# Scatter of the expert coefficients in two row tiles, and the weighing on VectorE straight out of PSUM

## The chip, the cores and the metric
The kernel runs on one core of one Trainium2 chip. The metric is the device time of one execution in microseconds (us), the median of the runs; lower is better.

## The reference, cut to what matters
Four stages follow each other on an activation of 4 x 256 tokens of 256 features: cross attention, a feed-forward layer with five-bit quantised weights, a gated expert layer with int8 quantisation, and a product-key expert layer. The change touches the last one alone.

```
q = (x @ Wq).reshape(b, t, H, 2, DK)                 # H=4 heads, DK=64
sim1 = einsum('bthd,hkd->bthk', q1, keys[:, :, 0])   # 128 keys a side
sim2 = einsum('bthd,hkd->bthk', q2, keys[:, :, 1])
s1, i1 = top_k(sim1, 8);  s2, i2 = top_k(sim2, 8)
all_scores  = s1[..., :, None] + s2[..., None, :]    # 8 x 8 pairs
all_indices = i1[..., :, None] * 128 + i2[..., None, :]
final_scores, pk_idx = top_k(all_scores, 8)
hidden = silu(x . e_down[idx]) * relu(final_scores)
out    = sum over 32 chosen experts of hidden * e_up[idx]
```

There are 2048 experts, and an index beyond them is clamped to the last.

## The kernel before, in words
The five engines run hand-written instruction lists, each in its own order, and meet at semaphores. The 1024 tokens are eight tiles of 128 (t = 0 to 7, `NT = 8`), two to a batch b (`B = 4`). The last expert layer gathers nothing. For each batch TensorE computes the inner product of every token with all 2048 rows of e_down, in eight steps called `experts`, and ScalarE writes silu of them as G (`gate`). An expert is numbered 16 x i + e, i from 0 to 127 and e from 0 to 15 (`EROWS`); G, and the coefficients PR, are laid out as [partition i, e, token].

The coefficients are made dense for a tile by one-hot matmuls, `scatter`. Before it VectorE has found each token's 32 choices (`top8`, `pair_top8`, `look_up`), and transposed them so that the 128 partitions are four slots of 32 tokens (s) times 32 choices, with 32 columns (g): token = 32 s + g. The coefficient is split in three bf16 parts whose sum is the f32 value. For each g, TensorE multiplies a stationary one-hot over i (`oh`, 128 x 128) with a moving one-hot over (slot, e), 4 x 16 = 64 columns, times the part (`wc`), and sums the three parts in PSUM: 96 matmuls a tile, in four quarters of 24, in banks 2 and 3 by turns. `slot16` adds 16 times the slot to the column index. `mask` and `one_hots` make msk (2048 elements a partition), oh (4096) and wc: two parts on VectorE, the third by `third_one_hots` on GpSimd.

For tiles 0 to 4 (`DVE_WEIGHS = NT - 3 = 5`) ScalarE copies each quarter out of PSUM into PR (`coefficients_out`, L1055) and GpSimd multiplies it by G (`weigh`, L381). For tiles 5 to 7 VectorE does both at once (L1495). Then `up` multiplies PR with e_up, sixteen matmuls (L728), and `result` adds the token's residual and lets it be stored.

These steps are woven with the gated expert layer (names with `c_`) of batch b + 2, whose steps go to and fro between TensorE, VectorE and ScalarE. The loop over b has two passes (b = 0 and 1); tiles 4 to 7 come behind it, the tail. TensorE's list in a pass: `sims(b, 1)`, `scatter(b, 0)`, `pre` (transposes of the next batch's tokens), `c_x_transposed`, `half_queries` (L668), `experts`, `c_factors`, `up(b, 0)`, ..., `sims(b + 1, 0)`, `c_first`, `scatter(b, 1)`, `experts`, ... , `up(b, 1)`. VectorE's: `top8`, `c_ratio` (first at L1309), `pair_top8`, `c_factor` (L1317), `look_up`, `c_round` (L1331), `mask`, `c_clip` (L1347), `one_hots`, `c_h`, `result`, `c_a`, then the same again for the next tile with `c_ratio2` (L1369), `c_factor2` (L1379), `c_round2`, `c_clip2` (L1352), and at the end `x3` and `ln_apply` (L1158). ScalarE: `tokens_out`, `queries`, `c_root` (L967), which `c_factor` waits for, `c_diag`, gates, and so on.

## Time and profile before

| | us |
|---|---|
| median of 3 runs | 459.7 (458.96 to 460.38) |
| profiled execution, its own time | 458.2 |
| span of its trace | 456.4 |
| TensorE matmuls busy | 374.5 (82%) |
| VectorE busy | 360.9 (79%) |
| ScalarE busy | 248.4 (54%) |
| GpSimd busy | 196.8 (43%) |

The numbers below are from one execution, in us from the start of its span. A row of a timeline merges neighbours of one kind: its start, its length, engine, line, operation, tiles and count; in square brackets stands the idle time of the engine before it and whose instruction ended it. An f32 matmul shows as two instructions, so x16 of them are eight calls. PE is TensorE, DVE is VectorE, ACT is ScalarE, POOL is GpSimd.

### The profile page before, as it was taken

How to read it: one execution, taken by the hardware profiler on the slowest of the kernel's cores; microseconds unless marked ns; L12 is line 12 of the kernel's file. 1: busy time of each engine (PE TensorE's matmuls, PEld its weight loads, DVE VectorE, ACT ScalarE, POOL GpSimd, SP SyncE). 2: the span in 40 equal slices, each digit the busy share in tenths (PEclk: the TensorE clock that was granted, in tenths of full speed). 3: DMA queues.
4: the chain of work that ended last, by engine and by line, in shares of the span. 5: the costliest groups of instructions: out<-in, count | busy, mean ns of one | idle time of the engine just before them, and what ended most of it. 6: DMA issues, size and time to landing. Idle time of an engine off the chain costs nothing.

```text
span 456.4 us, 6956 instructions
## 1 busy us (share of the span) xinstructions
PE 374.5 (82%) x2510; PEld 283.6 (62%) x2510; DVE 360.9 (79%) x878; ACT 248.4 (54%) x371; POOL 196.8 (43%) x211
## 2 busy tenths in 40 slices
PE   2987897599799988988388679978799878789486
PEld 1554664244345448987267568867688667688475
DVE  4998699958986956267947977698969799999991
ACT  4789959789788880136555254675475645012000
POOL 2355844479889993000011441353523325414220
PEclk9998999989989998998759968999999999979799
DMA  9910000000000004000000000000000000000000
GB/s 264 362 53 2 0 1 0 0 2 0 0 2 0 0 2 159 27 2 0 0 2 1 0 1 1 1 12 1 13 0 14 1 1 14 1 13 0 2 24 11
DMA packets 11138, 11.32 MB, mean 25 GB/s; under 512 B 608, under 2 KB 10592, under 8 KB 11104
## 3 DMA queue, kind: packets, MB, share of 16 engines
q1 hardware_dynamic: 11104, 10.88, 7.4%
q8 instruction: 20, 0.33, 0.3%
q14 instruction: 14, 0.11, 0.1%
HBM read 9.83 MB, written 1.05 MB: 24 GB/s over the span
## 4 chain that ended last, share of the span: by engine, by line
DVE 38%; PE 35%; ACT 13%; issue 9%; POOL 4%; DMA 1%; DVEq 0%; POOLq 0%; ACTq 0%
PE pair L728 6%; PE pair L559 5%; DVE arena L1480 5%; PE pair L697 5%; POOL arena L332 3%; PE pair L519 3%; PE pair L715 3%; PE pair L668 3%; PE pair L497 2%; PE pair L526 2%; DVE arena L1223 2%; DVE arena L1477 1%; DVE arena L1495 1%; PE pair L397 1%; DVE i L1422 1%
## 5 line engine op out<-in xcount | busy, mean ns | idle before, releaser
L332 POOL TENSOR_TENSOR arena<-arena 128x512 f32<-128x512 f32 x64 | 91.0, 1432 | 52.0 <-ACT arena L930 21.5
L697 PE MATMUL pair<-arena,EDT 128*128 128x256 f32 x256 | 59.5, 384 | 3.0 <-ACT arena L1063 3.0
L728 PE MATMUL pair<-EU,arena 128*128 128x256 f32 x256 | 57.8, 380 | 2.8 <-DVE arena L1502 1.6
L1223 DVE TENSOR_REDUCE arena<-arena 128x16 f32<-128x512 f32 x64 | 42.7, 679 | 20.2 <-POOL arena L332 20.1
L519 PE MATMUL pair<-QP,nidentr 128*128 128x512 f32 x144 | 47.6, 456 | 12.5 <-ACT arena L930 9.9
L369 POOL TENSOR_TENSOR arena<-arena,ctxT 128x2048 bf16<-128x2048 bf16 x8 | 34.8, 4351 | 46.9 <-DVE arena L1471 39.6
L697 PEld LDWEIGHTS pair<-arena,EDT 128*128 128x128 f32 x256 | 47.7, 191 | 9.9 <-ACT arena L1063 3.6
L728 PEld LDWEIGHTS pair<-EU,arena 128*128 128x128 f32 x256 | 47.9, 190 | 9.2 <-DVE arena L1495 3.1
L715 PE MATMUL pair<-arena 128*128 128x64 bf16 x768 | 30.4, 203 | 18.8 <-DVE arena L1495 9.4
L519 PEld LDWEIGHTS pair<-QP,nidentr 128*128 128x128 f32 x144 | 27.3, 203 | 24.4 <-issue 16.6
L1063 ACT ACTIVATE arena<-pair 128x512 f32<-128x512 f32 x32 | 18.7, 595 | 42.0 <-PE pair L697 41.9
L715 PEld LDWEIGHTS pair<-arena 128*128 128x128 bf16 x768 | 28.2, 104 | 21.5 <-DVE arena L1495 10.0
L381 POOL TENSOR_TENSOR arena<-arena 128x512 f32<-128x512 f32 x20 | 24.9, 1274 | 38.5 <-ACT arena L1055 38.5
L526 PE MATMUL pair<-arena 128*128 128x512 fp8e4 x128 | 40.4, 399 | 0.0
L933 ACT ACTIVATE arena<-pair 128x1024 f32<-128x1024 f32 x32 | 33.3, 1042 | 12.4 <-PE pair L526 12.4
L930 ACT ACTIVATE arena<-pair,sq_bias 128x1024 f32<-128x1024 f32 x32 | 36.2, 1131 | 5.9 <-PE pair L526 4.8
L1218 DVE TENSOR_SCALAR arena<-arena 128x1024 fp8e4<-128x1024 f32 x32 | 33.1, 1036 | 6.2 <-PE pair L526 3.7
L915 ACT ACTIVATE arena<-arena,clip_bias 128x1024 fp8e4<-128x1024 f32 x32 | 37.2, 1165 | 0.0
L559 PE MATMUL pair<-arena 128*128 128x128 f32 x256 | 32.8, 292 | 2.7 <-POOL arena L315 2.4
L559 PEld LDWEIGHTS pair<-arena 128*128 128x128 f32 x256 | 32.1, 208 | 3.5 <-issue 2.9
L497 PE MATMUL pair<-arena 128*128 128x512 f32 x64 | 30.9, 605 | 0.0
L1480 DVE TENSOR_TENSOR arena<-arena,ctxT 128x2048 bf16<-128x2048 bf16 x16 | 29.0, 1852 | 0.0
(196 smaller groups left out, 686.1 us busy)
## 6 DMA issues: line engine op xcount, KB each, us to landing
arena<-in_L_ffn_e_down_dram SPq DMA_DIRECT2D x1, 2048.0 KB, 12.2
EU<-in_L_ffn_e_up_dram SPq DMA_DIRECT2D x1, 2048.0 KB, 8.1
arena<-in_L_ffn_w_fc_dram SPq DMA_DIRECT2D x2, 512.0 KB, 5.3
X<-in_x_dram SPq DMA_DIRECT2D x1, 1024.0 KB, 6.0
arena<-in_L_ffn_w_proj_dram SPq DMA_DIRECT2D x1, 1024.0 KB, 13.7
GUW<-in_fside_BxS2xS_dram SPq DMA_DIRECT2D x1, 1024.0 KB, 11.4
out_dram<-arena SPq DMA_DIRECT2D x8, 128.0 KB, 1.7
CTX<-in_ctx_dram SPq DMA_DIRECT2D x1, 512.0 KB, 5.0
```

The lines of the kernel that those rows point to most:

```text
L332: pool.tensor_tensor(qf(g), sq[:, :, 0:32], sq[:, :, 32:64], ALU.add).then_inc(s["folded"], 1)
L497: last = pe.matmul(bank[2 + i % 2], W1T[:, k, m * P:m * P + P], xnT[:, k, half * 512:half * 512 + 512], start=(k == 0), stop=(k == 1))
L519: pe.matmul(to[half], nidentr[:, :], QP[:, c % 2, part, cols[half]], start=(part == 0), stop=False)
L526: last = pe.matmul(to[half], stepI[:, j, :], qr[:, g % QDEEP, cols[half]], start=False, stop=True, skip_group_check=kept)
L559: last = pe.matmul(bk2(F2_BANK[b])[:, n, o * P:o * P + P], h2T[:, k, at:at + P], W2T[:, k, o * P:o * P + P], start=(k == 0), stop=(k == HI ...
L697: last = pe.matmul(bk2(4 + i % 2)[:, r, :], EDT[:, k, at:at + P], xT4[:, b % 2, k, :], start=(k == 0), stop=(k == 1))
L715: last = pe.matmul(bank[2 + q % 2][:, g8 * 64:g8 * 64 + 64], oh[:, g // NG, :, g % NG], wc[:, c, g // NG, :, g % NG], start=(c == 0), stop ...
L728: last = pe.matmul(bk2(7)[:, n, :], PR[:, n, e, :], EU[:, e, :], start=(e == 0), stop=(e == EROWS - 1))
L915: act.activation(qr[:, g % QDEEP, :], qu[:, g // NS % 2, :], ACT.Relu, bias=clip_bias[:, 0:1], scale=-GRID / STEPS[g % NS], saturate=False ...
L930: act.activation(qd[g % 3], pair[2 + g % 2][:, :], ACT.Square, bias=sq_bias[:, g % NS:g % NS + 1]).then_inc(s["squared"], 1)
L1223: dve.tensor_reduce(err[:, g // NS % 2, :, g % NS], qf(g), AX.X, ALU.add).then_inc(s["reduced"], 1)
L1480: ins = dve.tensor_tensor(wc[:, c], msk, over(t, 2 + c, 64), ALU.mult)
```

## The change: what it does
- One scatter matmul becomes two, over partitions 0 to 63 and 64 to 127 of the same operands, each into a bank of its own. Each needs only its two slots, so the moving side is 2 x 16 = 32 columns (`JW`) in place of 64. A tile has 192 matmuls, in two halves of 96 with one wait ahead of each, in place of 96 in four quarters. `slot16` holds 0 or 16.
- msk shrinks to 1024 elements a partition, wc to 3 x 1024. VectorE makes all three parts of wc in one instruction; `third_one_hots` goes.
- `coefficients_out` (ScalarE) and GpSimd's `weigh` go. VectorE multiplies PSUM by G into PR for all eight tiles: two halves a tile, two instructions each.
- The second half of a tile goes into the banks of the first, so it waits for VectorE's products of the first half. For tiles 6 and 7 the second half has banks 4 and 5.
- The order: TensorE has `scatter(b, 0, 0)` before `pre`, and `scatter(b, 0, 1)` before `half_queries`; `scatter(b, 1, 1)` one `experts` step after its first half; in the tail `scatter(B-2, 1, 1)` stands inside `experts(B-1, 2..8)`. VectorE has `weigh(t, 0)` behind `top8` of the next tile and `weigh(t, 1)` behind its `pair_top8`.

```diff
-            def third_one_hots(t):
-                pool.wait_ge(s["d_mask"], t + 1)
...
-                pool.tensor_tensor(wc[:, 2], msk, part.unsqueeze(2).to_broadcast([P, NO, 64, NG]),
-                                   ALU.mult).then_inc(s["d_onehot_p"], 1)
...
+            def scatter(b, n, half):
                 t = 2 * b + n
+                if half == 0:
+                    pe.wait_ge(s["d_onehot"], t + 1)
+                if t == NT - 1:
+                    pe.wait_ge(s["d_weighed"], 4 * (t - 1) + 2 * half + 2)
+                elif t == NT - 2 and half == 1:
+                    pe.wait_ge(s["d_g_e"], 8 * B)
+                elif t or half:
+                    pe.wait_ge(s["d_weighed"], 4 * t + 2 * half)
+                for g16 in range(16):
+                    g = 16 * half + g16
+                    for c in range(3):
+                        for r in range(2):
+                            rows = slice(64 * r, 64 * r + 64)
+                            last = pe.matmul(bank[scatter_bank(t, half) + r][:, g16 * JW:g16 * JW + JW],
+                                             oh[rows, g // NG, :, g % NG], wc[rows, c, g // NG, :, g % NG],
+                                             start=(c == 0), stop=(c == 2))
+                last.then_inc(s["d_c_t"], 2)
...
-            def coefficients_out(t, quarters=range(4)):
...
-                    act.copy(pv[:, 8 * q:8 * q + 8], cv).then_inc(s["d_c_e"], 1)
...
             def one_hots(t):
...
-                for c in range(2):
-                    ins = dve.tensor_tensor(wc[:, c], msk, over(t, 2 + c, 64), ALU.mult)
+                dve.tensor_tensor(wc, msk.unsqueeze(1).to_broadcast([P, 3, NO, JW, NG]), parts, ALU.mult
+                                  ).then_inc(s["d_onehot"], 1)
...
+            def weigh(t, half):
...
+                dve.wait_ge(s["d_c_t"], 4 * t + 2 * half + 2)
+                for r in range(2):
+                    cv = bank[scatter_bank(t, half) + r][:, :].rearrange("p (g s e) -> p g s e", g=16, s=2)
+                    at = (slice(None), slice(16 * half, 16 * half + 16), slice(2 * r, 2 * r + 2))
+                    dve.tensor_tensor(pv[at], cv, gv[at], ALU.mult).then_inc(s["d_weighed"], 1)
```

First place: TensorE's list at the head of a pass of the loop, before. L715 is the scatter, L397 the transposes of `pre` and `c_x_transposed` (tokens XN), L668 `half_queries`; this is b = 0, and `s_d_c_e` is the count of ScalarE's copies.

```order
L715 MATMUL pair<-arena 128x64 [waits s_d_onehot_p,s_d_onehot]
L715 MATMUL pair<-arena 128x64 x47
L715 MATMUL pair<-arena 128x64 [waits s_d_c_e]
L715 MATMUL pair<-arena 128x64 x23
L715 MATMUL pair<-arena 128x64 [waits s_d_c_e]
L715 MATMUL pair<-arena 128x64 x23
L397 MATMUL pair<-ident,XN 128x128 [waits s_x3,s_ln4]
L397 MATMUL pair<-ident,XN 128x128 x3
L397 MATMUL pair<-ident,XN 128x128 [waits s_d_xT_e,s_x3,s_ln3]
L397 MATMUL pair<-ident,XN 128x128 x3
L668 MATMUL pair<-arena,WQ 128x256 [waits s_d_g_e,s_d_xT_e]
L668 MATMUL pair<-arena,WQ 128x256 x3
```

The same place after. L697 is the scatter, L377 the transposes, L648 `half_queries`.

```order
L697 MATMUL pair<-arena 128x32 [waits s_d_onehot]
L697 MATMUL pair<-arena 128x32 x95
L377 MATMUL pair<-ident,XN 128x128 [waits s_x3,s_ln4]
L377 MATMUL pair<-ident,XN 128x128 x3
L377 MATMUL pair<-ident,XN 128x128 [waits s_d_xT_e,s_x3,s_ln3]
L377 MATMUL pair<-ident,XN 128x128 x3
L697 MATMUL pair<-arena 128x32 [waits s_d_weighed]
L697 MATMUL pair<-arena 128x32 x95
L648 MATMUL pair<-arena,WQ 128x256 [waits s_d_g_e,s_d_xT_e]
L648 MATMUL pair<-arena,WQ 128x256 x3
```

The second half of the scatter moved behind the transposes and directly ahead of `half_queries`, and it waits for VectorE's count of products where it waited for ScalarE's count of copies.

Second place: VectorE's list in the second part of a pass, before, from `top8` (MAX and MAX_INDEX) over `c_ratio2` and `pair_top8` to `c_factor2`, which waits for ScalarE's root.

```order
L1416 MAX s<-pair 128x8 [waits s_d_sim_t]
L1416 MAX s<-pair 128x8 x7
L1422 MAX_INDEX i<-s,pair 128x8 [waits s_d_ranks,s_dve]
L1422 MAX_INDEX i<-s,pair 128x8 x7
L1369 TENSOR_REDUCE m_a<-pair 128x1 [waits s_c_aT_t]
...
L1437 MAX_INDEX pk<-fin,arena 128x8 x3
L1379 TENSOR_SCALAR sm<-sm 128x1 [waits s_c_root2,s_dve]
L1380 RECIPROCAL sm<-sm 128x1 [waits s_dve]
```

The same place after. L1469 is the product of PSUM with G; L1343 begins `c_ratio2`, L1353 is `c_factor2`.

```order
L1390 MAX s<-pair 128x8 [waits s_d_sim_t]
L1390 MAX s<-pair 128x8 x7
L1396 MAX_INDEX i<-s,pair 128x8 [waits s_d_ranks,s_dve]
L1396 MAX_INDEX i<-s,pair 128x8 x7
L1469 TENSOR_TENSOR arena<-pair,arena 128x16x2x16 [waits s_d_c_t,s_d_g_e]
L1469 TENSOR_TENSOR arena<-pair,arena 128x16x2x16
L1343 TENSOR_REDUCE m_a<-pair 128x1 [waits s_c_aT_t]
...
L1411 MAX_INDEX pk<-fin,arena 128x8 x3
L1469 TENSOR_TENSOR arena<-pair,arena 128x16x2x16 [waits s_d_c_t,s_d_g_e,s_dve]
L1469 TENSOR_TENSOR arena<-pair,arena 128x16x2x16
L1353 TENSOR_SCALAR sm<-sm 128x1 [waits s_c_root2]
```

Two products came in behind `top8` and two behind `pair_top8`; the steps of the gated layer that followed now stand behind them.

Third place: TensorE's list in the tail after, from `up(2, 0)` (the first L711) on. L661 is `sims(3, 1)`, L677 `experts`. Before, the whole scatter of tile 5 stood ahead of `sims` and the six `experts` steps were in one piece.

```order
L711 MATMUL pair<-EU,arena 128x256 [waits s_d_y,s_d_weighed]
L711 MATMUL pair<-EU,arena 128x256 x15
L697 MATMUL pair<-arena 128x32 [waits s_d_weighed,s_d_onehot]
L697 MATMUL pair<-arena 128x32 x95
L661 MATMUL pair<-keysT,arena 128x128 [waits s_d_simread,s_d_q_e]
L661 MATMUL pair<-keysT,arena 128x128 x7
L677 MATMUL pair<-arena,EDT 128x256 [waits s_d_g_e]
...
L677 MATMUL pair<-arena,EDT 128x256 x3
L697 MATMUL pair<-arena 128x32 [waits s_d_weighed]
L697 MATMUL pair<-arena 128x32 x95
L677 MATMUL pair<-arena,EDT 128x256 [waits s_d_g_e]
```

The second half of tile 5's scatter now stands behind three of the six steps.

## Rows read from the trace of the kernel before

**Rows 1.** Windows: length; busy PE, PEld, DVE, ACT, POOL; clock; DMA share; GB/s.

```profile
323.02:349.00 25.98, 24.66 (x215) 21.84 (x216) 20.90 (x69) 14.77 (x28) 9.92 (x11) 1.00 0.02 7
349.00:375.90 26.90, 21.10 (x207) 17.65 (x203) 23.19 (x75) 16.04 (x27) 9.97 (x11) 1.00 0.02 6
```

**Rows 2.** Timeline of VectorE, second pass of the loop.

```profile
323.35 1.68 DVE L1416 MAX8 s<-pair 128x8 f32<-128x128 f32 x8
...
327.22 0.69 DVE L1309 TENSOR_REDUCE m_xs<-pair 128x2 f32<-128x512 f32 x1
...
331.46 0.17 DVE L1317 TENSOR_SCALAR sm<-sm 128x2 f32<-128x2 f32 x1 [0.85 <-ACT sm L967]
...
342.27 0.86 DVE L1347 TENSOR_SCALAR arena<-arena 128x1024 bf16<-128x1024 bf16 x1 [3.11 <-ACT arena L996]
...
354.20 0.42 DVE L1369 TENSOR_REDUCE m_a<-pair 128x1 f32<-128x256 f32 x1 [0.54 <-PE pair L619]
...
365.73 1.91 DVE L1352 TENSOR_SCALAR arena<-arena 128x512 bf16<-128x512 bf16 x1 [1.92 <-ACT arena L1026]
...
369.77 2.35 DVE L1480 TENSOR_TENSOR arena<-arena,ctxT 128x2048 bf16<-128x2048 bf16 x2
```

**Rows 3.** Timeline of TensorE, second pass of the loop.

```profile
323.10 1.82 PE L715 MATMUL pair<-arena 128*128 128x64 bf16 x48 [1.51 <-ACT arena L1055]
...
327.01 3.62 PE L668 MATMUL pair<-arena,WQ 128*128 128x256 f32 x16
...
333.92 1.05 PE L588 MATMUL pair<-arena,ones 128*128 128x128 f32 x8
...
346.16 1.16 PE L681 MATMUL pair<-keysT,arena 64*128 64x128 f32 x16
```

**Rows 4.** Groups of instructions by line and shape, 285 to 457 us.

```profile
L1495 DVE TENSOR_TENSOR arena<-pair,arena 128x512 f32<-128x512 f32 x12 | 13.0, 1116 | 1.7 <-PE pair L715 1.7
...
L1471 DVE TENSOR_TENSOR arena<-arena,ctxT 128x2048 bf16<-128x2048 bf16 x7 | 8.5, 1217 | 0.1
...
L1331 DVE TENSOR_TENSOR arena<-XN,pair 128x512 f32<-128x512 f32 x1 | 0.7, 687 | 0.1
```

**Rows 5.** Timeline of VectorE around the start of the loop's first pass.

```profile
257.14 5.76 DVE L1480 TENSOR_TENSOR arena<-arena,ctxT 128x2048 bf16<-128x2048 bf16 x2
...
268.44 0.17 DVE L1156 RECIPROCAL rstd<-rstd 128x2 f32<-128x2 f32 x1 [2.95 <-ACT rstd L856]
...
269.29 1.68 DVE L1416 MAX8 s<-pair 128x8 f32<-128x128 f32 x8
```

**Rows 6.** Timeline of GpSimd there: the third part of wc for tile 0.

```profile
255.10 5.59 POOL L369 TENSOR_TENSOR arena<-arena,ctxT 128x2048 bf16<-128x2048 bf16 x1 [4.04 <-DVE arena L1471]
```

**Rows 7.** Timeline of TensorE, the loop's first pass.

```profile
262.96 3.69 PE L715 MATMUL pair<-arena 128*128 128x64 bf16 x72 [4.14 <-DVE arena L1480]
...
272.20 5.63 PE L668 MATMUL pair<-arena,WQ 128*128 128x256 f32 x16
```

**Rows 8.** Window inside that `half_queries`; columns as in rows 1.

```profile
272.40:275.00 2.60, 2.60 (x8) 2.06 (x7) 2.46 (x14) 0.00 (x0) 0.24 (x1) 0.50 0.00 0
```

**Rows 9.** Timeline of TensorE, the tail.

```profile
379.36 3.72 PE L668 MATMUL pair<-arena,WQ 128*128 128x256 f32 x16 [1.07 <-ACT arena L1041]
...
395.45 1.63 PE L715 MATMUL pair<-arena 128*128 128x64 bf16 x48
...
434.20 7.14 PE L728 MATMUL pair<-EU,arena 128*128 128x256 f32 x32 [1.59 <-DVE arena L1502]
...
446.59 7.17 PE L728 MATMUL pair<-EU,arena 128*128 128x256 f32 x32 [1.25 <-DVE arena L1495]
```

**Rows 10.** Timeline of VectorE, the tail.

```profile
376.24 1.68 DVE L1416 MAX8 s<-pair 128x8 f32<-128x128 f32 x8
...
404.37 0.41 DVE L1427 TENSOR_TENSOR arena<-s 128x256 f32<-128x256 f32 x1
...
412.89 5.77 DVE L1480 TENSOR_TENSOR arena<-arena,ctxT 128x2048 bf16<-128x2048 bf16 x2
```

More of the change, by code:

```diff
@@ L54, in build @@
     NO = 32 // NG
+    JW = 2 * EROWS
     QDEEP = 8
@@ L224, in build, with scatter_bank @@
             d_xT_t d_xT_e d_q_t d_q_e d_sim_t d_simread d_ranks d_final d_parts d_packed d_mask d_onehot
-            d_onehot_p d_c_t d_c_e d_g_t d_g_e d_weighed d_up_t d_y stored0 stored1""".split()
+             d_c_t d_g_t d_g_e d_weighed d_up_t d_y stored0 stored1""".split()
         s = {n: sem("s_" + n) for n in names}
         block = ctx.enter_context(nc.Block())
-        DVE_WEIGHS = NT - 3
         DVE_ROUNDS = 2
+        def scatter_bank(t, half):
+            return 4 if t >= NT - 2 and half else 2
         def cbank(b):
@@ L699, in experts @@
                     last.then_inc(s["d_g_t"], 1)
-            def scatter(b, n):
+            def scatter(b, n, half):
                 t = 2 * b + n
-                pe.wait_ge(s["d_onehot"], t + 1)
-                pe.wait_ge(s["d_onehot_p"], t + 1)
-                for q in range(4):
-                    u = 4 * t + q
-                    if u - 2 >= 4 * DVE_WEIGHS:
-                        pe.wait_ge(s["d_weighed"], u - 1)
-                    elif u >= 2:
-                        pe.wait_ge(s["d_c_e"], u - 1)
-                    for g8 in range(8):
-                        g = 8 * q + g8
-                        for c in range(3):
-                            last = pe.matmul(bank[2 + q % 2][:, g8 * 64:g8 * 64 + 64], oh[:, g // NG, :, g % NG], wc[:, c, g // NG, :, g % NG],
+                if half == 0:
[13 more added lines that the diff above has]
+                                             oh[rows, g // NG, :, g % NG], wc[rows, c, g // NG, :, g % NG],
                                              start=(c == 0), stop=(c == 2))
-                    last.then_inc(s["d_c_t"], 1)
+                last.then_inc(s["d_c_t"], 2)
             def up(b, n, lo, hi_):
@@ L776, in _ @@
                 sims(b, 1)
-                scatter(b, 0)
+                scatter(b, 0, 0)
                 pre(b + 1)
                 c_x_transposed(b + 2)
+                scatter(b, 0, 1)
                 half_queries(b + 1, 0, 2)
@@ L789, in _ @@
                 c_first(b + 2)
-                scatter(b, 1)
+                scatter(b, 1, 0)
                 experts(b + 1, 4, 5)
                 c_a_transposed(b + 2)
+                scatter(b, 1, 1)
                 experts(b + 1, 5, 7)
@@ L804, in _ @@
             sims(B - 2, 1)
-            scatter(B - 2, 0)
+            scatter(B - 2, 0, 0)
             pre(B - 1)
+            scatter(B - 2, 0, 1)
             half_queries(B - 1, 0, 2)
@@ L810, in _ @@
             up(B - 2, 0, 0, EROWS)
-            scatter(B - 2, 1)
+            scatter(B - 2, 1, 0)
             sims(B - 1, 1)
-            experts(B - 1, 2, 8)
+            experts(B - 1, 2, 5)
+            scatter(B - 2, 1, 1)
+            experts(B - 1, 5, 8)
             up(B - 2, 1, 0, EROWS)
             for n in range(TPB):
-                scatter(B - 1, n)
+                scatter(B - 1, n, 0)
+                scatter(B - 1, n, 1)
                 up(B - 1, n, 0, EROWS)
@@ L1046, in queries @@
                     act.copy(qT4[:, b % 2, 2 * i:2 * i + 2, :], bk2(4 + i)).then_inc(s["d_q_e"], 1)
-            def coefficients_out(t, quarters=range(4)):
-                if t >= 2:
-                    act.wait_ge(s["d_up_t"], t - 1)
-                pv = PR[:, t % 2, :, :].rearrange("p e (s g) -> p g s e", s=4)
-                for q in quarters:
-                    act.wait_ge(s["d_c_t"], 4 * t + q + 1)
-                    cv = bank[2 + q % 2][:, :].rearrange("p (g s e) -> p g s e", g=8, s=4)
-                    act.copy(pv[:, 8 * q:8 * q + 8], cv).then_inc(s["d_c_e"], 1)
             def gate(b, lo, hi_):
@@ L1575, in _ @@
             top8(NT - 3)
+            weigh(NT - 4, 0)
+            pair_top8(NT - 3)
+            weigh(NT - 4, 1)
             for t in (NT - 3, NT - 2):
-                pair_top8(t)
+                if t == NT - 2:
+                    pair_top8(t)
                 look_up(t)
```

59 lines of the change are left out of this document (19 added, 40 removed).

## The prediction

> **What bounds the kernel now.** I read the page's busy shares first, then windows of the last stage, then the timelines of the engines side by side, and last the groups by shape for prices. In the second pass of the loop (323 to 376 us) VectorE is busy 20.9 + 23.2 = 44.1 of 52.9 us and TensorE 45.8 [rows 1]: neither is full, and ScalarE and GpSimd are far from it. The timeline shows why: work goes to and fro, and VectorE's waits all end on a step of the gated layer, 0.85 us on ScalarE's root, 3.11 on its integers, 0.54 on TensorE's transposes, 1.92 on the second integers [rows 2]. What counts is therefore when `half_queries` starts, for ScalarE makes the queries before the root, and `c_factor` at 331.46 follows `half_queries` at 327.01 by 4.45 us [rows 2, 3]. Before, the copies on ScalarE and the products on GpSimd lie beside VectorE's `top8`, and delay TensorE by 1.51 us [rows 3].
>
> **Prices.** A product of 128 x 512 from PSUM takes 1.10 us or a little less back to back [rows 4]; I take 1.075 and 2.15 for a half tile (called W below). It could fall to 0.69, what 512 f32 elements with a PSUM operand take in another layout [rows 4]; I keep the first, since it is the same operation with the same stride in PR and G.
>
> wc: two instructions of 2048 elements take 2.35 us beside no GpSimd work [rows 2], and the smaller mask instruction of 2048 takes 1.22 [rows 4]. At the same rate, about 0.55 us per 1024, one of 3072 takes 1.75 and the mask 0.65. For tile 0 and, in the tail, tiles 5 and 6, the two instructions took 5.76 and 5.77 [rows 5, 10], because GpSimd's third part ran at the same time and stretched to 5.59 itself [rows 6]. That collision goes: 4.0 us each. `c_clip2` has 512 elements and takes 1.91 beside that GpSimd work [rows 2]; I take 0.2, so 1.7 goes.
>
> Scatter: 48 matmuls with 64 columns take 1.63 us, of which the last one's own length is 0.2, so 30 ns each [rows 9]. Nothing before shows 32 bf16 columns in two row tiles. The nearest are `sims`, f32 matmuls over 64 partitions by turns in the two halves: 16 instructions of 128 columns in 1.16 us, against 8 f32 instructions of 128 columns over all 128 partitions in 1.05 [rows 3]. Without the last one's 0.3 that is 57 against 107 ns: two row tiles do run beside each other. From below, both profits together (half of 30 for the tiles, half again for the columns) give 8 ns; from above, no profit, 30. I take 18, a little over the 15 that the tiles alone would give, because each matmul also has its own weight load. A half of 96 is then 1.75 us plus 0.2 until VectorE may read (1.0 to 3.1).
>
> A rule of the Trainium skill speaks against this value. The page "TensorE: Matmul & The Clock Gate", section "Wait — 56ns, not 53.3ns?", says that matmuls never start closer together than about 25 ns, however few their columns. By that a half takes 2.4 us. The closest starts in this trace are 30 ns apart, so it doesn't show whether the floor exists; the rival below gives what 25 would do.
>
> **Second pass of the loop (times from the start of its `top8`, 323.35).** Before, `c_ratio` starts at 3.87, `half_queries` at 3.66, `c_factor` at 8.11 [rows 2, 3]. After, VectorE does `top8` to 3.87 and W to 6.02. The second half of the scatter stands in TensorE's list directly ahead of `half_queries` and waits for this W; all of TensorE waits behind it. It runs to 7.87, `half_queries` starts there, 4.2 us later than before, and `c_factor` comes at 12.3. VectorE alone would be ready at 11.5 (3.87, two W, and the 3.4 of `c_ratio` and `pair_top8`), so this wait ends on ScalarE and the second W is hidden. From here to the next `top8` the chain is as before and carries the 4.2: the products fill none of the 3.11, since no product stands there. Then W stands before `c_ratio2` (+2.15, less the 0.54 of waiting that it covers: +1.6) and the other before `c_factor2` (+2.15; ScalarE's root is long done). The mask is hidden in the wait that follows. `c_clip2` gives back 1.7, wc 0.6. Sum: 4.2 + 1.6 + 2.15 - 1.7 - 0.6 = +5.6 us. TensorE itself waits some 4 us for its `scatter(b, 1, 1)`, but is not late for anything after it: it has about 1 us in hand at `c_factors2`.
>
> **First pass.** Here the start comes earlier: wc 4.0 and the mask 0.55 sooner, and ScalarE's `std` no longer stands behind two copies, of the 2.95 us wait about 0.35 is left [rows 5]: 7.1 in all. `top8` starts at 262.2 and not at 269.3. `half_queries` follows 7.87 later, at 270.1, against 272.2 before [rows 7]: -2.1. The rest of the pass is that of the second without its 4.2: +1.4. Sum -0.7.
>
> **Tail (times as if its first `top8` still began at 376.24).** `half_queries` starts at 384.1, 4.75 late [rows 9, 10]. TensorE's list to the scatter of tile 5 is full, so that its first half runs from 400.2 to 402.0 (before 395.45 [rows 9]). The second half stands behind `sims` (1.05) and three `experts` steps (each four calls of the kind of which `up` does sixteen in 7.1, so 5.2 in all [rows 9]): 408.2 to 410.0. VectorE's second W on tile 5 ends at 412.3, where before its products were done at 404.37 [rows 10]: +7.95. Then wc without the collision gives back 4.0 and two masks 1.1; the products of tile 6 are four in 4.3 and their scatter is long done, where before they waited for quarters (0.6 more). TensorE's `up(3, 0)` comes at 436.0 instead of 434.2 [rows 9]. Then `up` 7.0, half a scatter 1.95, and two W, 4.3 (the second half of the scatter hides under the first W): the last `up` starts at 449.4 instead of 446.59 [rows 9]: +2.8.
>
> **The clock.** In the first pass of before TensorE waited 4.14 us, scattered, and its `half_queries` then took 5.63 us at a granted clock of 0.50, that is 1.2 GHz [rows 7, 8], where that of the second pass took 3.62 at 2.4 GHz [rows 3]. After the change it waits over 4 us (the transposes end at about 1.6, W at 6.0) ahead of `half_queries` in the second pass and in the tail as well, and about 10 us ahead of `up(3, 0)` (scatter of tile 6 done at some 426, `up` at 436). I price each at the 2.0 us between the two rows: +6.0. The first pass pays this already.
>
> **Sum.** -0.7 + 5.6 + 2.8 + 6.0 = +13.7 us on the profiled execution's own 458.2 (span 456.4 and 1.8 around it), 471.9. That execution lies 1.5 under the median of 459.7, which gives 473.
>
> ScalarE loses 20 copies, GpSimd 20 products and 8 third parts of wc. What they held up is in the terms above; the rest ran beside other work on engines that were waiting anyway, and I count it at nothing.
>
> **Rivals.**
> 1. *No profit from row tiles*, 30 ns a matmul. Six halves lie on the path (one in each pass, four in the tail, the last one hidden under W): 6 x 1.15 = +6.9, 480. For it: each matmul has a weight load as large as before. Against: `sims`. The 25 ns of the page, a rival of the same kind, gives 6 x 0.67 = +4, 477.
> 2. *The clock doesn't fall* in the new waits, because the small matmuls and transposes break them: 467. If the scatter also takes 8 ns, 6 x 0.96 less: 461.
> 3. *Faster.* VectorE's product costs 0.7 us in its new shape and not 1.075. Twelve W are on the path (three in each pass, six in the tail), each 0.75 cheaper: -9. With a scatter at 8 ns (-5.8) and one fall of the clock left (-4): 473 - 19 = 454. It decides from about 0.8 us per product on. Against it: twelve rows at 1.10 in the old order of the same strides.
> 4. *The removed GpSimd work never delayed VectorE*, and the 5.76 us have another cause: then the 4.0 come back for tiles 0 and 6 (for tile 5 VectorE waits for the scatter anyway), and 1.7 in each pass: +11.4, 484. Against it: GpSimd's row starts and ends around VectorE's in all three.
>
> **How the numbers follow.** Forecast 473 with its neighbours from 468 to 478: 0.45. Rival 1 with the page's floor 0.22; the clock rival 0.17; faster 0.09; near no change (461 and the like) 0.04; rival 4 0.03. The range that leaves out no more than 2 in 10 goes from 462 to 483. What a measurement of this kernel can tell from no change is 0.3%, 1.4 us: faster 0.10, within 0.04, slower 0.86.
>
> **What would show it.** In the profile after: L1469 thirty-two times near 1.07 us; L697 1536 matmuls, a half in 1.7 us; the wc instruction near 1.75 for every tile and no large GpSimd work in the last stage; TensorE idle for 4 us or more, ended by VectorE's L1469, ahead of the second half of each even tile; `half_queries` 7.9 us behind the start of `top8`; the loop's second pass near 58.5 us long instead of 52.9. The forecast falls if `half_queries` follows `top8` by under 6 us, or if the pass stays at 53.

## The result: 1.9% slower

The kernel after takes 468.29 us (median of 4 runs, 467.17 to 469.14), the kernel before, run beside it, 459.33 (4 runs, 456.59 to 460.38). The ratio is 1.0194, 95% interval 1.0152 to 1.0236. The forecast was 473.0 with a range of 462 to 483: sign and range hold, and of +13.7 us there were +9.0. The kernel before itself ran between 453.8 and 461.5 us in all, with medians of 456.2 to 459.3 beside the five groups of runs told of here, so two ratios taken in different groups are not told apart below some 0.7%.

The page of the kernel after: the span, the busy time of each engine, and two of its groups (out<-in, count | busy us, mean ns | idle just before, and what ended most of it).

```profile
span 465.4 us, 8442 instructions
...
PE 373.5 (80%) x3278; PEld 279.0 (60%) x3278; DVE 351.4 (76%) x890; ACT 229.7 (49%) x351; POOL 136.2 (29%) x183
...
L1469 DVE TENSOR_TENSOR arena<-pair,arena 128x512 f32<-128x512 f32 x32 | 32.5, 1063 | 11.7 <-PE pair L697 11.6
...
L697 PE MATMUL pair<-arena 64*128 64x32 bf16 x1536 | 22.3, 177 | 23.5 <-DVE arena L1469 20.6
```

The thirty-two products cost about what they cost before, 1.06 us for 1.12 [rows 4]. The second group shows where the price of the change lies: TensorE stood idle for 23.5 us right before a scatter, 20.6 of them until VectorE had made a product, where before it was 18.8 and 9.4. Busy time hides this, since VectorE is 76% busy and TensorE 80%.

TensorE, second pass of the loop (start, us, instruction, what ended the idle time before it):

```profile
325.42 1.46 PE L697 MATMUL pair<-arena 64*128 64x32 bf16 x96 [4.04 <-DVE arena L1469]
326.81 4.68 PE L648 MATMUL pair<-arena,WQ 128*128 128x256 f32 x16
...
356.48 1.46 PE L697 MATMUL pair<-arena 64*128 64x32 bf16 x96 [4.20 <-DVE arena L1469]
357.88 4.51 PE L677 MATMUL pair<-arena,EDT 128*128 128x256 f32 x16
```

And in the tail:

```profile
383.68 1.46 PE L697 MATMUL pair<-arena 64*128 64x32 bf16 x96 [5.44 <-DVE arena L1469]
385.08 4.56 PE L648 MATMUL pair<-arena,WQ 128*128 128x256 f32 x16
...
423.21 1.87 PE L697 MATMUL pair<-arena 64*128 64x32 bf16 x136
426.39 0.86 PE L697 MATMUL pair<-arena 64*128 64x32 bf16 x56 [1.31 <-issue]
436.86 9.39 PE L711 MATMUL pair<-EU,arena 128*128 128x256 f32 x32 [9.61 <-DVE arena L1475]
446.19 2.26 PE L697 MATMUL pair<-arena 64*128 64x32 bf16 x167
450.03 0.49 PE L697 MATMUL pair<-arena 64*128 64x32 bf16 x25 [1.57 <-issue]
452.73 10.01 PE L711 MATMUL pair<-EU,arena 128*128 128x256 f32 x32 [2.21 <-DVE arena L1469]
```

`half_queries` (L648) starts 7.29 us behind `top8` in the pass and 7.30 in the tail, where before it was 3.66 and 3.12 [rows 2, 3, 9, 10]. The matmuls behind a long wait are slow: 4.68 against 3.62, and the last two `up`s (L711) 9.39 and 10.01 against 7.14 and 7.17 [rows 9]. The clock in three windows of these, columns as in [rows 1]:

```profile
327.00:331.00 4.00, 4.00 (x15) 3.38 (x16) 3.52 (x14) 0.59 (x1) 1.20 (x5) 0.78 0.02 4
437.00:446.00 9.00, 9.00 (x32) 7.44 (x32) 3.58 (x2) 0.00 (x0) 0.00 (x0) 0.75 0.04 15
453.00:462.50 9.50, 9.50 (x32) 7.72 (x32) 0.00 (x0) 0.00 (x0) 0.00 (x0) 0.71 0.00 0
```

A mean of 0.78, 0.75 or 0.71 is a step that begins at 1.2 GHz (0.50) and ends at 2.4 (1.00): finer windows of the first have 0.50 from 327 to 328 us and 1.00 from 329 to 331.

VectorE after, at the start of the loop and in the second pass:

```profile
255.50 1.75 DVE L1454 TENSOR_TENSOR arena<-arena,ctxT 128x3072 bf16<-128x3072 bf16 x1
...
261.05 1.67 DVE L1390 MAX8 s<-pair 128x8 f32<-128x128 f32 x8
...
319.52 1.67 DVE L1390 MAX8 s<-pair 128x8 f32<-128x128 f32 x8
...
323.36 2.00 DVE L1469 TENSOR_TENSOR arena<-pair,arena 128x512 f32<-128x512 f32 x2
...
328.54 2.05 DVE L1469 TENSOR_TENSOR arena<-pair,arena 128x512 f32<-128x512 f32 x2
332.25 0.17 DVE L1291 TENSOR_SCALAR sm<-sm 128x2 f32<-128x2 f32 x1 [1.66 <-ACT sm L956]
...
369.49 0.29 DVE L1326 TENSOR_SCALAR arena<-arena 128x512 bf16<-128x512 bf16 x1 [2.48 <-ACT arena L1015]
```

`c_factor` comes 332.25 - 319.52 = 12.73 us behind `top8`, where it came 8.11 behind it [rows 2], and ends a wait on ScalarE's root of 1.66 (0.85 before). With the collision gone, wc is 1.75 and `c_clip2` 0.29 (5.76 and 1.91 before [rows 2, 5]).

The time by stage, each from the start of its first `top8` (the tail to the start of the last `result`), for before, after, and two experiments told of below:

| | before | after | row tiles only | the same, kept busy |
|---|---|---|---|---|
| first pass begins at | 269.29 | 261.05 | 261.64 | 261.06 |
| first pass | 54.06 | 58.47 | 53.88 | 50.47 |
| second pass | 52.89 | 58.26 | 54.39 | 50.21 |
| tail | 77.56 | 84.99 | 80.36 | 73.65 |

After against before: -8.2, +4.4, +5.4, +7.4, together +9.0. Of the -8.2, 1.1 lie ahead of the changed steps: `look_up` of tile 0 begins at 250.89 before and at 249.78 after, and between 249.8 and 251.3 in other versions with the same instructions up to there.

### The profile page after: what moved, and what is told of

Same layout as the page of the kernel before. It is cut to its first block, busy times and chain, and to the rows that moved or that the text cites. A ratio compares the mean times of both kernels' runs of the same rounds, so it can differ in the third digit from the quotient of the medians.

```text
span 465.4 us, 8442 instructions
## 1 busy us (share of the span) xinstructions
PE 373.5 (80%) x3278; PEld 279.0 (60%) x3278; DVE 351.4 (76%) x890; ACT 229.7 (49%) x351; POOL 136.2 (29%) x183
## 4 chain that ended last, share of the span: by engine, by line
PE 38%; DVE 37%; ACT 11%; issue 9%; POOL 4%; DMA 1%; DVEq 0%; POOLq 0%; ACTq 0%
PE pair L711 9%; PE pair L677 6%; PE pair L539 5%; DVE arena L1469 4%; PE pair L648 4%; POOL arena L335 3%; PE pair L499 3%; DVE i L1396 3%; PE pair L477 2%; DVE s L1390 2%; PE pair L697 2%; PE pair L506 2%; DVE arena L1197 2%; DVE arena L1454 1%; DVE arena L1450 1%
## 5 line engine op out<-in xcount | busy, mean ns | idle before, releaser
L335 POOL TENSOR_TENSOR arena<-arena 128x512 f32<-128x512 f32 x64 | 90.7, 1427 | 52.6 <-ACT arena L922 21.4
L711 PE MATMUL pair<-EU,arena 128*128 128x256 f32 x256 | 62.9, 404 | 11.8 <-DVE arena L1475 9.6
L677 PE MATMUL pair<-arena,EDT 128*128 128x256 f32 x256 | 61.4, 391 | 3.0 <-ACT arena L1043 3.0
L711 PEld LDWEIGHTS pair<-EU,arena 128*128 128x128 f32 x256 | 51.5, 205 | 19.6 <-DVE arena L1469 12.0
L677 PEld LDWEIGHTS pair<-arena,EDT 128*128 128x128 f32 x256 | 48.6, 195 | 10.3 <-ACT arena L1043 3.6
L353 POOL CAST i12f<-i 128x64 bf16<-128x64 uint32 x8 | 2.0, 252 | 147.4 <-DVE i L1396 147.4
L1469 DVE TENSOR_TENSOR arena<-pair,arena 128x512 f32<-128x512 f32 x32 | 32.5, 1063 | 11.7 <-PE pair L697 11.6
L697 PE MATMUL pair<-arena 64*128 64x32 bf16 x1536 | 22.3, 177 | 23.5 <-DVE arena L1469 20.6
L697 PEld LDWEIGHTS pair<-arena 64*128 64x128 bf16 x1536 | 21.0, 96 | 26.8 <-DVE arena L1469 22.0
L539 PE MATMUL pair<-arena 128*128 128x128 f32 x256 | 30.7, 280 | 2.7 <-POOL arena L318 2.4
L539 PEld LDWEIGHTS pair<-arena 128*128 128x128 f32 x256 | 30.1, 197 | 3.5 <-issue 2.9
L318 POOL TENSOR_TENSOR arena<-arena 128x512 f32<-128x512 f32 x16 | 22.2, 1385 | 0.0
## 6 DMA issues: line engine op xcount, KB each, us to landing
arena<-in_L_ffn_w_proj_dram SPq DMA_DIRECT2D x1, 1024.0 KB, 13.6
GUW<-in_fside_BxS2xS_dram SPq DMA_DIRECT2D x1, 1024.0 KB, 11.4
```

Of the source, the lines that this page charges most:

```text
L335: pool.tensor_tensor(qf(g), sq[:, :, 0:32], sq[:, :, 32:64], ALU.add).then_inc(s["folded"], 1)
L539: last = pe.matmul(bk2(F2_BANK[b])[:, n, o * P:o * P + P], h2T[:, k, at:at + P], W2T[:, k, o * P:o * P + P], start=(k == 0), stop=(k == HI ...
L677: last = pe.matmul(bk2(4 + i % 2)[:, r, :], EDT[:, k, at:at + P], xT4[:, b % 2, k, :], start=(k == 0), stop=(k == 1))
L697: last = pe.matmul(bank[scatter_bank(t, half) + r][:, g16 * JW:g16 * JW + JW], oh[rows, g // NG, :, g % NG], wc[rows, c, g // NG, :, g % N ...
L711: last = pe.matmul(bk2(7)[:, n, :], PR[:, n, e, :], EU[:, e, :], start=(e == 0), stop=(e == EROWS - 1))
L1469: dve.tensor_tensor(pv[at], cv, gv[at], ALU.mult).then_inc(s["d_weighed"], 1)
```

## The experiments

Each ratio is to the kernel before, run beside it on the same chip. My theory: the products' places in VectorE's list hold up TensorE and the gated layer, and the waits that this makes cost again through the clock. Rivals: the row tiles bring nothing; the engines' sums set the time; the slow matmuls have another cause than the clock.

**The change in two halves.** First, row tiles and three parts of wc on VectorE, with the copies on ScalarE and the products on GpSimd kept for tiles 0 to 4:

```diff
-                elif t or half:
+                elif 4 * t + 2 * half > 4 * DVE_WEIGHS:
                     pe.wait_ge(s["d_weighed"], 4 * t + 2 * half)
+                elif t or half:
+                    pe.wait_ge(s["d_c_e"], 4 * t + 2 * half)
...
-                weigh(t, 0)
                 c_ratio(b + 2)
                 pair_top8(t + 1)
-                weigh(t, 1)
```

> The row tiles and the wc instruction of the changed kernel, with the copies on ScalarE and the products on GpSimd kept for tiles 0 to 4 (two copies a half). Theory (the products on VectorE and TensorE's wait for them are the whole loss, the row tiles and the three parts on VectorE are a gain): first top8 of the loop near 261 us as after the change, a pass of the loop 50 to 51 us (52.9 before, 58.3 after), the tail 78 to 80 us, in all about 447 us. Rival (the scatter in 192 small matmuls, its instruction stream and its waits cost the time): passes of 55 us or more and 463 us or more.

Measured: 454.91 us, ratio 0.9945 (0.9911 to 0.9978). Faster than before, but by a quarter of what was expected. By stage the whole gain is the earlier start (-7.65), which comes with the third part of wc off GpSimd; the passes and the tail are -0.2, +1.5 and +2.8. TensorE in its second pass:

```profile
317.86 0.63 PE L392 MATMUL pair<-ident,XN 128*128 128x128 f32 x4 [1.87 <-ACT arena L1047]
318.42 1.38 PE L714 MATMUL pair<-arena 64*128 64x32 bf16 x96
319.73 5.32 PE L663 MATMUL pair<-arena,WQ 128*128 128x256 f32 x16
...
352.72 0.71 PE L620 MATMUL pair<-arena,ones 128*128 128x128 f32 x4 [1.92 <-ACT arena L987]
354.63 3.78 PE L692 MATMUL pair<-arena,EDT 128*128 128x256 f32 x8 [1.20 <-ACT arena L1069]
358.20 3.06 PE L728 MATMUL pair<-EU,arena 128*128 128x256 f32 x8
```

Behind waits of 1.87 and 1.92 us (the latter 1.03 before) TensorE's steps are cold: 5.32 where 3.62 is warm [rows 3], 3.78 and 3.06 where 1.9 is. Its last two `up`s took 9.47 and 9.90. The row tiles save time and the clock takes it back; the versions kept busy, below, show that. Why one wait of 1.87 ahead of `half_queries` made cold what waits of 1.51 and 1.16 left warm before, no run shows.

Second, the products on VectorE in the places of the kernel after, with the old scatter and GpSimd's third part:

```diff
+                for q in (2 * half, 2 * half + 1):
+                    u = 4 * t + q
+                    if u >= 2:
+                        pe.wait_ge(s["d_weighed"], u - 1)
```

> The other part alone: 64-column scatter in quarters and GpSimd's third part of wc as before, but all products on VectorE and TensorE's list as in the changed kernel. Theory: everything that the products cost and nothing of what the smaller wc gives back: a pass near 61 us, the collision of wc with GpSimd (5.8 us for tile 0) still there, in all 476 to 482 us. Rival (row tiles are the loss): about 460 us.

Measured: 479.38, ratio 1.0456 (1.0374 to 1.0538); its passes are 60.95 and 61.16 and its tail 88.3. So the moved products alone cost 4.6%, the row tiles with all of wc on VectorE give 0.5%, and both are at 1.9%. The second half of the change is worth more beside the first: put on top of the products it takes 6.0 us off the start and 8.7 off the passes and the tail; put on the kernel before it takes 7.65 off the start and adds 4.1 to the rest. That this is so because the scatter then stands in a chain with the products is my reading and not shown.

**The third part back on GpSimd**, everything else as after:

```diff
+                pool.tensor_tensor(wc[:, 2], msk, part.unsqueeze(2).to_broadcast([P, NO, JW, NG]),
+                                   ALU.mult).then_inc(s["d_onehot_p"], 1)
...
-                dve.tensor_tensor(wc, msk.unsqueeze(1).to_broadcast([P, 3, NO, JW, NG]), parts, ALU.mult
+                dve.tensor_tensor(wc[:, 0:2], msk.unsqueeze(1).to_broadcast([P, 2, NO, JW, NG]), parts, ALU.mult
```

> The changed kernel with the third part of wc (now 1024 elements) back on GpSimd, as before the change. Theory (VectorE and GpSimd hold each other up over SBUF): GpSimd's instruction takes about 1.9 us alone; VectorE's oh or wc beside it is stretched by about that for tiles 0, 5, 6 where it follows the mask at once, in the passes of the loop VectorE's wait for ScalarE hides it; in all 1 to 3 us slower than the changed kernel. Rival (no collision, the third part was well placed): 1 to 2 us faster, since VectorE's wc falls from 1.75 to 1.2 us.

Measured: 469.32, ratio 1.0252 (1.018 to 1.0323). VectorE's wc of tile 0, then that of tile 2:

```profile
256.67 2.92 DVE L1467 TENSOR_TENSOR arena<-arena,ctxT 128x2048 bf16<-128x2048 bf16 x1
...
315.93 1.22 DVE L1467 TENSOR_TENSOR arena<-arena,ctxT 128x2048 bf16<-128x2048 bf16 x1
```

GpSimd's part at tile 0 and at tile 2:

```profile
254.63 3.88 POOL L372 TENSOR_TENSOR arena<-arena,ctxT 128x1024 bf16<-128x1024 bf16 x1 [3.50 <-DVE arena L1456]
...
311.13 1.90 POOL L372 TENSOR_TENSOR arena<-arena,ctxT 128x1024 bf16<-128x1024 bf16 x1 [7.17 <-DVE arena L1456]
```

The same two instructions take 2.92 and 3.88 side by side, 1.22 and 1.90 apart. The collision is real: the rival that gave the 5.76 us another cause is out. The ratio alone couldn't show its price; by stage, against after, the start is 2.3 later, the tail 1.2 longer and the passes 0.6 and 0.3 shorter.

**The place in VectorE's list**: the first half's product ahead of `top8`.

```diff
-                top8(t + 1)
                 weigh(t, 0)
+                top8(t + 1)
```

> The changed kernel with the first products of a tile ahead of the next tile's top8 in VectorE's list, nothing else. Theory (TensorE is held behind products that stand after top8): half_queries about 4 us behind the loop's ln_apply and not 7.6, but c_factor then waits for VectorE's own work, so a pass shortens by 1.4 us only; in the tail the waits of 4.4 and 5.3 us for tile 5's scatter shrink by about 4; in all about 461 us. Rival (VectorE's added work alone sets the time, the place of the products is of no account): 466 to 469 us.

Measured: 463.49, ratio 1.0121 (1.0052 to 1.0189), 0.7% under after in its own ratio, though the intervals overlap. In the second pass `half_queries` is warm (3.72; in the first pass and the tail it took 4.61 and 5.36), TensorE's waits for the products shrink to 0.24 and 0.40, and `c_factor` comes 9.10 behind `top8`. But now TensorE waits elsewhere, 2.18 us for ScalarE's L963 with an `up` of 8.76 behind it, and 4.72 for L970 ahead of `c_factors2`. The second pass stays at 58.39; the profit is in the tail (80.7).

**The place in TensorE's list**: `half_queries` ahead of the second half of the scatter.

```diff
-                scatter(b, 0, 1)
                 half_queries(b + 1, 0, 2)
+                scatter(b, 0, 1)
```

> The kernel after, with one line of TensorE's list moved: half_queries stands ahead of the second half of the scatter of the even tile, and so no longer waits for VectorE's product. The prediction gave this wait 4.2 us per pass. If it is what holds up the gated layer, half_queries starts some 3 us behind top8's start instead of 7.3, and the second products wait for the scatter behind it (about 8 us behind top8's start), which lies under c_ratio and pair_top8. VectorE's own list (top8 3.87, two half tiles 4.1, c_ratio and pair_top8 3.4) then allows c_factor at 11.4 where it stood at 12.7. So 1.3 us less per pass and the same in the tail, and half_queries no longer cold: about 464 where the kernel after is at 468.3, ratio 1.01. Rival: TensorE's list is the whole cause; then c_factor comes back to 8 to 9, 4 us less per pass, 457 and a ratio of 1.00.

Measured: 459.05, ratio 1.0013 (0.9976 to 1.005): with this one line the whole loss is gone. These are the same instructions in another order, so the rival that the engines' sums set the time is out. In the profiled execution the passes are 56.61 and 55.87 and the tail 79.70, that is -1.9, -2.4 and -5.3 against after. Against before they are still 2.6, 3.0 and 2.1 longer: the earlier start (-7.7) pays for that. VectorE, second pass:

```profile
318.22 1.68 DVE L1390 MAX8 s<-pair 128x8 f32<-128x128 f32 x8
...
327.28 2.06 DVE L1469 TENSOR_TENSOR arena<-pair,arena 128x512 f32<-128x512 f32 x2
329.25 0.16 DVE L1291 TENSOR_SCALAR sm<-sm 128x2 f32<-128x2 f32 x1
```

`c_factor` (L1291) stands 11.03 us behind `top8`, with no wait before it: as worked out (11.4), in the loop VectorE's own list is then the bound, and of the 4.6 us that `c_factor` had lost only 1.7 come back. The time is that of the expectation's rival all the same. In the tail, where no gated layer follows, TensorE's list decides, and there I had expected too little:

```profile
375.23 3.72 PE L648 MATMUL pair<-arena,WQ 128*128 128x256 f32 x16 [0.67 <-ACT arena L1030]
380.05 1.37 PE L697 MATMUL pair<-arena 64*128 64x32 bf16 x96 [1.10 <-DVE arena L1469]
...
385.89 7.07 PE L711 MATMUL pair<-EU,arena 128*128 128x256 f32 x32
```

The first `up` stands 11.80 behind `top8` (374.09) and not 17.18 as after (394.96 - 377.78). Not all of it is the wait itself: `half_queries` took 3.72 for 4.56, and the last two `up`s 8.54 and 9.70 for 9.39 and 10.01.

**The clock.** The kernel after, with matmuls whose result nobody reads put into its waits:

```diff
+            def keep_busy(to, n):
+                for e in range(n):
+                    pe.matmul(to, ident[:, :], EU[:, e % EROWS, :], start=True, stop=True)
...
+                pe.wait_ge(s["d_simread"], NT)
+                keep_busy(bk2(0)[:, 0, :], (20, 5)[n])
                 up(B - 1, n, 0, EROWS)
```

> The kernel after, plus f32 matmuls of 128x256 whose result nobody reads, put where TensorE waits for VectorE: 8 ahead of the second half of the scatter of each tile in the loop, 10 in the tail ahead of the same place, 20 ahead of the next to last up and 5 ahead of the last up. Clock theory: the waits themselves cost what they cost, and TensorE's fall to 1.2 GHz costs more on top. Then half_queries takes 3.6 us and not 4.7 (three times 1.1), the next to last up 7.1 and not 9.4, the last 7.1 and not 10.0: 8.5 us less than the kernel after, some 457 where the kernel before is at 456.9, i.e. a ratio near 1.00. Rival: the slow steps have other causes (operands, bank conflicts) or the extra matmuls run into the waits' ends: no change from the kernel after, ratio 1.02. A third way: a part of the gain, because a step that is warm only moves the wait to VectorE.

Measured: 465.34, ratio 1.0178 (1.0089 to 1.0266). All the slow steps became fast, but the extra matmuls ran on past the end of the waits, by 1.0 and 1.3 us ahead of the last two `up`s and by 0.9 ahead of `half_queries` in the second pass (in the first, where they ran cold themselves, by 2.5):

```profile
428.54 10.59 PE L705 MATMUL pair<-EU,ident 128*128 128x256 f32 x40
438.96 7.07 PE L716 MATMUL pair<-EU,arena 128*128 128x256 f32 x32
```

VectorE's products for that `up` were done at 437.62, and the `result` that frees its bank, from 437.53 on, took 0.41: the `up` could have started at 437.94. So, with fewer (`(16, 3)[n]`, and 5 and 7 for 8 and 8 in the loop):

> The kernel after with extra matmuls as in the earlier one, but fewer (5, 7, 10, 16 and 3 calls where there were 8, 8, 10, 20 and 5), since the earlier one's trace shows that they ran on past the end of the wait by 1.0 us in each pass and by 1.3 us ahead of each of the last two ups. If the clock is worth what the rows say, the time falls by these 4.6 us from 465.3, to 461, ratio to before 1.007 to 1.01. Rival: with fewer of them the steps are cold again, and it stays at 465, ratio 1.018.

Measured: 461.81, ratio 1.0077 (1.0038 to 1.0117), the time that the clock theory gave. The last two `up`s:

```profile
438.35 7.14 PE L716 MATMUL pair<-EU,arena 128*128 128x256 f32 x32 [2.92 <-DVE arena L1488]
...
451.09 7.17 PE L716 MATMUL pair<-EU,arena 128*128 128x256 f32 x32 [0.96 <-DVE arena L1482]
```

All of the profit lies in the tail (78.17 against 84.99: 2.25 and 2.84 for the two `up`s, 0.84 for `half_queries`, 0.9 for the gap told of below). The passes stay at 58.9 and 58.6. In the first, the extra matmuls ran cold and past the wait, so that `half_queries` was warm but stood 8.33 behind `top8` (7.26 after); in the second, 1.91 us of wait were left behind them and it took 4.97 all the same:

```profile
265.19 4.47 PE L705 MATMUL pair<-EU,ident 128*128 128x256 f32 x10
...
327.44 1.43 PE L697 MATMUL pair<-arena 64*128 64x32 bf16 x96 [1.91 <-DVE arena L1482]
```

What the clock costs within a pass of the kernel after is thus read from rows and not shown by undoing it.

The same 20 and 5 ahead of the last two `up`s of the version with row tiles alone:

> The version in which only the row tiles and the three parts on VectorE come in, with the copies on ScalarE and the products on GpSimd kept, plus the 20 and 5 matmuls ahead of the last two ups alone. The ups took 9.47 and 9.90 us in it without them. Clock theory: each takes 7.1, so 2.4 + 2.8 = 5.2 us less than its 454.9, a ratio to the kernel before of 0.984. Rival: the extra matmuls, which lie behind the scatter in TensorE's list, run on past the moment at which the products are ready; then the gain is 2 us or less, ratio 0.991 or more.

Measured: 449.44, ratio 0.9823 (0.9736 to 0.991). Both `up`s came to 7.14 and 7.17. With more in the loop's waits as well:

```diff
                 pre(b + 1)
+                pe.wait_ge(s["d_g_e"], 8 * b + 8)
+                keep_busy(bk2(4)[:, 0, :], 3)
                 c_x_transposed(b + 2)
...
                 experts(b + 1, 5, 7)
+                pe.wait_ge(s["d_y"], 2 * b + 1)
+                keep_busy(bk2(7)[:, 1, :], 4)
                 c_factors2(b + 2)
+                keep_busy(bk2(7)[:, 1, :], 2)
                 experts(b + 1, 7, 8)
```

> The version with row tiles and three parts on VectorE, copies and products where they were, and the extra matmuls ahead of the last two ups; now also inside the loop, where TensorE waits: three calls behind the transposes ahead of half_queries, four ahead of c_factors2 and two behind it. Each call takes 0.44 us at 2.4 GHz. In the version without them half_queries took 5.4 us, the experts step behind c_factors2 3.8 and the next up step 3.1; at 2.4 GHz they take 3.7, 1.9 and 1.9. Clock theory: 4.7 us of TensorE's work less in each of the two passes; since VectorE and ScalarE set part of the pass, some 2 to 4 us less per pass, so the time falls from 449.4 to about 443, ratio to before 0.966 to 0.975. Rival: the calls overrun the waits or the steps that get faster are not on the path: 448 to 450, ratio 0.98.

Measured: 442.08, ratio 0.9632 (0.9577 to 0.9686), the fastest version here, 3.7% under before. Its passes and tail:

```profile
261.10:311.50 50.40, 48.80 (x627) 41.98 (x628) 40.83 (x141) 30.87 (x53) 14.22 (x20) 1.00 0.02 4
311.50:361.70 50.20, 48.63 (x627) 41.73 (x627) 40.66 (x141) 30.84 (x54) 14.63 (x20) 1.00 0.02 7
361.70:435.80 74.10, 69.06 (x966) 59.28 (x965) 54.30 (x164) 10.55 (x16) 11.14 (x22) 1.00 0.03 9
```

The clock is full throughout, and TensorE (with the extra matmuls) fills 48.6 of 50.2 us. The control, the kernel before with such matmuls in its own waits:

> A control for the fastest version: the kernel before, with nothing of the change, and with matmuls whose result nobody reads in its own waits (eight calls ahead of the scatter of tile 0, where TensorE waits 4 us; two behind the transposes, two ahead of c_factors2 and two behind it in each pass). Its only cold steps of size are half_queries of the first pass (5.6 us against 3.6) and what stands around it. If the fastest version's gain came from the extra matmuls alone, this one would gain as much, 4%. My theory is that the extra matmuls only give back what the clock takes once the shorter scatter leaves TensorE idle: here they give 0 to 3 us, ratio 0.993 to 1.00. Rival: 0.97.

Measured: 456.66, ratio 0.9983 (0.9947 to 1.002). In the loop the extra matmuls bring little by themselves: the passes are 52.74 and 52.80, where they were 54.06 and 52.89, and 50.47 and 50.21 in the fastest version. There they let the row tiles' profit through. Ahead of the last two `up`s the control has none, and in its profiled execution `up(3, 0)` was cold (7.14 before [rows 9]):

```profile
431.07 9.56 PE L733 MATMUL pair<-EU,arena 128*128 128x256 f32 x32 [1.56 <-DVE arena L1514]
```

So this `up` is warm in one execution and cold in another behind much the same waits (5.75 and 1.56 us of TensorE just before it, 5.27 and 1.59 in the kernel before), and what extra matmuls at that place would give the kernel before is untested. These rows allow 2.4 us (0.5%) at this `up`, against the 3.7% of the fastest version.

**The row tiles**: all 48 matmuls of one row tile, then all 48 of the other.

```diff
-                for g16 in range(16):
+                for r, g16 in [(r, g16) for r in range(2) for g16 in range(16)]:
                     g = 16 * half + g16
                     for c in range(3):
-                        for r in range(2):
```

> The kernel after, with the 96 matmuls of a half in another order: all 48 of the first row tile, then all 48 of the second, where they alternated. If the 12.5 ns per matmul come from two row tiles that run beside each other, each matmul now has to wait for the one before it in its own row tile: 25 to 30 ns each, 2.4 to 2.9 us for a half where it was 1.37. Eight halves or so on the path: 5 to 10 us slower than the kernel after, ratio to before 1.03 to 1.04. Rival: the narrow matmul (32 columns) alone makes the 12.5 ns; then a half stays at 1.4 us and the time at that of the kernel after, 1.02.

Measured: 478.5, ratio 1.0455 (1.0361 to 1.0549). A half takes 2.48 us (2.65 cold) and not 1.36 (1.46):

```profile
320.94 2.48 PE L696 MATMUL pair<-arena 64*128 64x32 bf16 x96
329.23 2.65 PE L696 MATMUL pair<-arena 64*128 64x32 bf16 x96 [3.83 <-DVE arena L1468]
```

Less about 0.17 for the last one's own length (192 by turns in one burst take 2.57, twice 1.36 less 0.15), that is 2.31 / 95 = 24 ns a matmul in one row tile and 1.19 / 95 = 12.5 ns by turns. The time went past the 10 us expected, for `half_queries` is colder too (5.73).

**The gap.** After, the 192 matmuls of tiles 6 and 7 stop for 1.31 and 1.57 us on nothing that the profile knows. With the third part left out of these two tiles' scatter (128 matmuls each):

```diff
-                    for c in range(3):
+                    for c in range(3 if t < NT - 2 else 2):
```

> The kernel after, with the third part of the coefficients left out of the scatter of the last two tiles alone (128 matmuls each instead of 192; the output loses those parts). After, the 192 matmuls of a tile ran with a gap of 1.3 to 1.6 us that nothing in the profile ends, after 136 and 167 of them. If the gap is TensorE's stream of instructions that runs dry in a long burst of short ones, a burst of 128 ends before it: the gap is gone, and the scatter takes about 1.7 us instead of 4.0 and 4.3. Rival: the gap has to do with the place in the program or with the bank: it stays, 1.3 us or more. In time it is 1 to 2 us either way for the last tile, since part of the next to last tile's scatter is hidden.

Measured: 465.78, ratio 1.0184 (1.0094 to 1.0275). The gap is gone:

```profile
424.30 1.77 PE L697 MATMUL pair<-arena 64*128 64x32 bf16 x128
437.95 9.43 PE L711 MATMUL pair<-EU,arena 128*128 128x256 f32 x32 [11.89 <-DVE arena L1475]
447.31 1.77 PE L697 MATMUL pair<-arena 64*128 64x32 bf16 x128
```

That fits a stream of instructions that runs dry in a long burst, and so do the smaller gaps with one row tile after the other, at 24 ns a matmul (0.31 and 0.40). It isn't shown: in the fastest version 192 ran through in 2.57 and 2.56 us. Its cause stays open. It costs little in any case, since the first one is hidden.

## Why the prediction was right, and what was mis-sized

- *The wait takes the place of the copies.* Right, and shown from both sides: `half_queries` began 7.3 us behind `top8` (forecast 7.9), and moving it ahead of that wait took the loss back, though in the loop 1.7 us of `c_factor`'s 4.6 only; the rest is VectorE's own list. TensorE's other wait, 4.20 us ahead of `scatter(b, 1, 1)`, was foreseen as harmless, and is: `c_factors2` starts 1.13 us behind `c_factor2`, as before, though the `experts` steps between were cold too (4.51).
- *The scatter*, taken at 18 ns a matmul and 1.75 us a half: 12.5 ns and 1.36 to 1.46. It was the term with the widest bounds (8 to 30), and the rows of `sims` spoke for less than I took. Rival 1 (30 ns) is out. The Trainium skill's page "TensorE: Matmul & The Clock Gate", section "Wait — 56ns, not 53.3ns?", gives about 25 ns as the least from one start to the next. The trace disagrees with that floor for two row tiles by turns (12.5), and agrees with it for one at a time (24).
- *The product*, 1.075: 1.063. W came to 2.0 to 2.1. Rival 3 (0.7 us) is out.
- *The start of the first pass*, -7.1: -8.2. The collision gave its 4.0, as forecast. The other 1.1 stood there ahead of the changed steps: the term was right, and the total is that much lower without the change's doing.
- *Each pass* was forecast at +5.6 and 2.0 for the clock in the second, and at 7.1 - 0.7 = 6.4 in the first; measured +5.4 and +4.4. In the first, `half_queries` stood 7.26 behind `top8` (7.87 forecast) and took 4.91, not the 5.63 of before that the forecast kept. In the second, `c_factor` was to lose 12.3 + 2.0 - 8.11 = 6.2 us and lost 4.6: half a microsecond from the scatter and W, and 1.0 from the clock. `half_queries` after the wait took 4.68, not 5.6, because the clock came back midway; I had taken the price from the one cold row there was [rows 7, 8]. From there, W ahead of `c_ratio2` cost 1.3 (forecast 1.6) and ahead of `c_factor2` 1.6 (2.15), and the steps to the next `top8` gave back 2.2 (2.3). The sign "near 58.5" for this pass was worked out without the clock's 2.0; that 58.3 met it is luck. Of the 4.7 us by which the sum was too high, 5.3 are in the start and the passes, and the tail was 0.6 too low.
- *The tail*, +2.8 and 4.0 for two cold steps: +7.4. `up(3, 0)` came 1.1 late with 0.8 of the clock in it (forecast 1.8 without the clock), and the last `up` 4.6 late, of which 3.1 are the clock's: without it the tail was +1.5. Cheaper halves of the scatter took more off than a gap of 0.9 put on. The clock's cost lay otherwise: 0.8 for `half_queries`, 2.25 for `up(3, 0)`, and 2.84 for the last `up`, which I had not priced. It follows a scatter of small matmuls, a gap and a wait of 2.21.
- *The clock* over all, +6.0: the rows of after give 1.1 + 0.8 + 2.3 + 2.8 = 7.0. The first pass's `half_queries` gives 0.7 of that back. The size was right by luck: two cold steps priced too high and one not priced cancel. By these rows some 6.3 of the +9.0 are the clock and 2.7 the rest, where the forecast had 6.0 and 7.7 (an estimate that takes each of these steps to be wholly on the path). Its rival (the clock doesn't fall) is out; the shortened keep-busy run shows 6.8 us of tail for it and the gap.
- *What I missed*: in the prediction every shorter scatter was pure profit. The version with row tiles and without the moved products shows cold steps in both passes, 1.7 + 1.9 + 1.2 us in the second, and kept busy it is 3.4 and 4.2 shorter there.

## What to carry to other kernels

Before an operation moves to another engine, read which instruction stands behind its consumer in the next engine's list: here a product of 2 us, placed late, held up a step that had nothing to do with it, and one swapped line was worth as much as the whole loss. Where TensorE gets faster without being the bound, look at the clock in what follows its new gaps; here matmuls without use in these waits turned a gain of 0.5% into 3.7%, and such matmuls in the waits of the kernel before's loop gave nothing that its time shows. Size them to the wait by the trace: here an overrun of 1.1 us ate most of the 1.2 that a warm `half_queries` saved.
